# Query weights split one tile earlier, down scales folded into a weight copy, and gate blocks in banks of their own

## The chip, the cores and the metric

The kernel runs on one core of a Trainium2 chip. A core has five engines that work at the same time and meet only at semaphores: TensorE (PE, matrix products into PSUM), VectorE (DVE), ScalarE (ACT), GpSimd (POOL), and SyncE (SP), which here issues every load and store. PSUM has eight banks of 128x512 float32. The metric is the device time of one execution in microseconds, lower is better. Before the change the median of three runs is 315.86 us (315.81 to 316.04).

## The reference

A gated cross attention layer and a gated feed forward layer, over 16 batches of 64 tokens with 256 features:

```
h   = layernorm(x);  q = h@wq;  k, v = h@wk, h@wv;  kc, vc = ctx@wk_ctx, ctx@wv_ctx
q, k = rope(rms_norm(q)*q_w), rope(rms_norm(k)*k_w);  kc = rms_norm(kc)*k_w
p   = softmax(q@[kc,k].T/sqrt(128) + causal mask)       # 16 query heads, 4 key heads
x1  = x + tanh(g_xattn) * (p@[vc,v]).reshape(...)@wo
h2  = layernorm(x1)
a   = silu((h2@fp8(gate_w))*gate_scale) * ((h2@fp8(up_w))*up_scale)     # 768 wide
out = x1 + tanh(g_ffn) * (a@fp8(down_w))*down_scale
```

fp8() rounds a weight to e4m3 and back to float32. The float32 accuracy has to be kept.

## The kernel before

**Tiles and steps.** The tokens are eight tiles of 128 rows (two batches each), and each tile has four head groups. One pair (tile, group) is a step, so there are 32 steps, 0 to 31, and seven more (32 to 38) in which the pipeline drains. Step k is tile k // 4, group j = k % 4. Each engine has its own function `one_step`, and the order of the work is the order in which these functions are written. In step k PE turns the rotated queries of step k (L609), projects the queries of step k + 1 (L625 or L628), applies the output weights to the attention of step k - 2 (`output_projection`), multiplies queries and keys of step k (L664), turns the probabilities of step k - 1 (L676), projects one kind of key or value of the next tile (`keys_values`), does one piece of a feed forward (`FF_LATE`: pieces 0, 1, 2 and the down product of tile t in steps 4t+6 to 4t+9) and ends with the attention product of step k - 1 (L708).

**The softmax loop.** Beside PE there is a loop through the other engines: ACT copies the turned queries (`qt`, L817), squares the projected ones (L739), DVE rotates them (L1035, L1039), takes the row maximum of the scores (L1168) and makes `exp_bias` (L1171), ACT does the exponentials (L897), then the copy of the attention output (`ot_raw` or `ot_hi`, L806 and L810), and again `qt`.

**Native and split weights.** A float32 product by PE is either native (operands as they are, `one_pass`, L411) or split: weight and token matrix are each cut into a high part that is exact in fp32r and a low remainder, and three products (hi x hi, hi x lo, lo x hi; `high_passes` and `low_passes`, L400 and L405) are added up. `NATIVE_TILES` says how many of the first tiles use native products for each kind of weight; later tiles use the split ones. `SPLIT_AT` says in which step a weight chunk is split: ACT copies the high part (`split_weights`, L727, between `pt` and the exponentials of that step), DVE subtracts it from the raw chunk (L957, between `ssq_eps` and `row_inv`). PE waits at the first use for `w_lo_ready`.

**Rounding.** The six feed forward chunks are rounded to e4m3 by DVE (`rounding_constant`, `round_weights`, `out_of_range`), one in each step of `ROUND_AT`. For the two chunks of the down weights POOL writes the result to `w_down` one step later (`quantize_store`, L1315). The first down product, in step 9, waits for both (L532).

**The last tile.** Its feed forward runs in steps 34 to 37. Gate and up blocks of a piece share a bank, its three pieces have the banks ps_f, ps_k, ps_s. ACT makes tanh of the gate block (L793), DVE multiplies it by the gate block (L1051) and by the up block and `fuse_scale` (L1061, two instructions of 128x128), PE does the down product native (L540), DVE multiplies by the row `down_rows` (L1070) and adds x (L1074), and SP stores the tile.

Of the kernel before, what the change touches and what calls it, by code (L numbers as in the profile page):

```python
# [45 lines left out]

NATIVE_TILES = {"kv": (3, 3, 3, 3), "q": (3, 3, 3, 3), "o": (3, 3, 3, 3)}
SPLIT_AT = {5: [("kv", 0)], 6: [("kv", 1)], 7: [("kv", 2)], 9: [("kv", 3)], 10: [("q", 0)], 11: [("q", 1)],
            12: [("q", 2), ("o", 0)], 13: [("q", 3)], 14: [("o", 1)], 15: [("o", 2)], 16: [("o", 3)]}
SPLIT_ORDER = [c for at in sorted(SPLIT_AT) for c in SPLIT_AT[at]]  # L50
ROUND_AT = {0: 0, 1: 1, 2: 2, 3: 3, 4: 4, 8: 5}
NAN_AT = 4
# [8 lines left out]

SHORT_OF_VECTOR = (3,)

# [26 lines left out]
def build(nc, x, ctx_in, wq, wk, wv, wo, wk_ctx, wv_ctx,  # L90
# [5 lines left out]
    with ExitStack() as stack:  # L96
# [6 lines left out]
        def sem(name):  # L103
            return stack.enter_context(nc.semaphore(name))
# [22 lines left out]
        with nc.sbuf_tensor("kv_raw", [P, 4, KC, GW], f32) as kv_raw, \  # L127
# [10 lines left out]
        w_ff = sb("w_ff", [P, 2, KC, FF], f16)  # L138
        w_down = sb("w_down", [P, FC, HID], f32r)
        quant_m = sb("quant_m", [P, FF])  # L140
        ff_peak = sb("ff_peak", [P, WIDE])
# [53 lines left out]


        ident_in, const_in, rows_in, small_in, down_rows_in, x0_in, x1_in, x_in = (
            sem(n) for n in ("ident_in", "const_in", "rows_in", "small_in", "down_rows_in", "x0_in", "x1_in", "x_in"))
# [30 lines left out]
        ff_made, tanh_ready, gated_ready, fuse_ready, fuse_hi_ready, fuse_lo_ready = (  # L229
            sem(n) for n in ("ff_made", "tanh_ready", "gated_ready", "fuse_ready", "fuse_hi_ready", "fuse_lo_ready"))  # L230
        down_made, down_scaled, result_ready = sem("down_made"), sem("down_scaled"), sem("result_ready")

# [162 lines left out]
        def _(pe):  # L395
# [97 lines left out]
            def spread_nan(u, k):  # L493

                if at_step(u, k) == NAN_AT:
# [5 lines left out]
                    last.then_inc(nan_spread, 1)  # L501

            def feed_forward(u, slot):

# [3 lines left out]
                if piece is not None:  # L508
# [7 lines left out]
                    elif piece > 0 and ff_bank(u, ff_m, piece) is ps_f:  # L516
                        pe.wait_ge(fuse_ready, tile(u, ff_m) * 3 + piece)
                    bank_f = ff_bank(u, ff_m, piece)
                    blocks = ((0, 2 * piece), (0, 2 * piece + 1), (1, 2 * piece), (1, 2 * piece + 1))
                    for a in range(2):  # L520
# [202 lines left out]
        def _(act):  # L723
# [60 lines left out]
            def tanh_gate(u, slot):  # L784

                ff_m, piece = slot or (None, None)
                if piece is not None:
                    act.wait_ge(ff_made, tile(u, ff_m) * 3 + piece + 1)
                    if isinstance(u, int) and tile(u, ff_m) == 0 and piece == 0:
# [151 lines left out]
        def _(dve):  # L941
# [77 lines left out]
            def down_row_scale():  # L1019
# [4 lines left out]
                                        ALU.mult, ALU.add).then_inc(scales_ready, 1)  # L1024

            def rotate_queries(u, k):

# [14 lines left out]
            def gate_and_fuse(u, slot):  # L1042
# [4 lines left out]
                if piece is not None:  # L1047
# [9 lines left out]
                    elif piece == 0 and is_tile(u, ff_m - 1):  # L1057
                        dve.wait_ge(result_ready, tile(u, ff_m))
                    for i in range(2):
                        c = 2 * piece + i  # L1060
# [5 lines left out]
                if piece is None:  # L1066
                    dve.wait_ge(down_made, tile(u, ff_m) + 1)
                    if not last_tile(u, ff_m):
                        dve.wait_ge(fuse_lo_ready, tile(u, ff_m) * 3 + 3)
                    nc.vector.tensor_tensor(down_y, ff_bank(u, ff_m, piece)[:, 0:HID], down_rows[:, :], ALU.mult)\  # L1070
                        .then_inc(down_scaled, 1)
                    if last_tile(u, ff_m):
                        dve.wait_ge(down_scaled, tile(u, ff_m) + 1)
                        nc.vector.tensor_tensor(x_tile(u, ff_m), down_y, x_tile(u, ff_m), ALU.add)\  # L1074
                            .then_inc(result_ready, 1)

# [11 lines left out]
            def one_step(u, k):  # L1088
# [122 lines left out]

                split_weights(u, k)

                if at_step(u, k) in ROUND_AT:
# [265 lines left out]
```

## Time and profile before

| | |
|---|---|
| median of three runs | 315.86 us |
| profiled execution, its own time | 316.00 us |
| its span, first to last instruction | 314.0 us |
| PE busy (weight loads) | 296.9 us, 95% (233.1 us) |
| DVE, ACT, POOL busy | 229.0, 232.0, 182.3 us |
| granted clock of PE | full in all 40 slices |

Busy shares of all 314 us say little here, since PE, and the loop through ACT and DVE, take turns at setting the pace. The chain of waits, in order of time, tells which does so in which step. DMA is done with its large loads after the first four of 40 slices (some 31 us) and moves little afterwards. Records of PE overlap a little, since ends of matmuls are modelled, so in the chain a piece is counted from the end of the piece before it.

### The profile page before, as it was taken

What the parts mean: (1) busy time and instruction counts of PE and PEld (TensorE: products, weight loads), DVE (VectorE), ACT (ScalarE), POOL (GpSimd) and SP (SyncE); (2) the same over time, 40 slices, a digit from 0 to 9 for tenths busy, and PEclk for the clock granted to TensorE, in tenths of its full rate; (3) what the DMA queues carried; (4) which work ended last, traced back from release to release, by engine and by line L of the source; (5) the groups of instructions that cost most, each with busy time, mean ns of one, the idle gap of its engine ahead of it and who ended that gap; (6) DMA issues with size and microseconds to landing.
All of it is one profiled execution on the core that took longest, in us unless ns stands there. A gap on an engine that the chain in (4) does not pass through costs nothing.

```text
span 314.0 us, 6534 instructions
## 1 busy us (share of the span) xinstructions
PE 296.9 (95%) x2223; PEld 233.1 (74%) x2223; DVE 229.0 (73%) x478; ACT 232.0 (74%) x892; POOL 182.3 (58%) x177
## 2 busy tenths in 40 slices
PE   7897989998999899999999999999999999987976
PEld 3344656666767678878888888888888888786864
DVE  1668998889759976769887787758765865576554
ACT  2468688777878678897999768896888678776622
POOL 1235685577646877346975586457755684456230
PEclk9999999999999999999999999999999999999999
DMA  6999000000000010000100010000000000000001
GB/s 197 395 390 380 8 17 2 0 1 11 8 2 2 0 35 2 0 0 3 34 2 0 2 37 0 2 1 20 0 3 0 2 18 3 0 2 17 2 0 35
DMA packets 6721, 12.84 MB, mean 41 GB/s; under 512 B 801, under 2 KB 4257, under 8 KB 6689
## 3 DMA queue, kind: packets, MB, share of 16 engines
q1 hardware_dynamic: 6688, 12.43, 11.1%
q8 instruction: 18, 0.29, 0.4%
q14 instruction: 15, 0.11, 0.1%
HBM read 11.38 MB, written 1.05 MB: 40 GB/s over the span
## 4 chain that ended last, share of the span: by engine, by line
PE 35%; ACT 25%; DVE 22%; issue 8%; POOL 6%; DMA 2%; SPq 1%; DVEq 0%; POOLq 0%
ACT probs L897 9%; ACT squares L739 6%; PE ps_y L437 5%; DVE row_max L1168 4%; PE ps_attn L708 3%; DVE exp_bias L1171 3%; PE ps_scores L664 3%; PE ps_transposed L423 3%; DVE q_sin L1039 3%; PE ps_q L411 3%; ACT qt L817 3%; PE ps_ff L525 3%; PE ps_probs L423 2%; DVE q_rot L1035 2%; PE ps_kv L411 2%
## 5 line engine op out<-in xcount | busy, mean ns | idle before, releaser
L897 ACT ACTIVATE probs<-ps_scores,exp_bias,q_scale 128x128 f32<-128x128 f32 x128 | 56.9, 455 | 24.1 <-DVE exp_bias L1171 24.1
L1343 POOL TENSOR_TENSOR q_rot<-q_rot,q_sin 128x512 f32<-128x512 f32 x31 | 39.7, 1279 | 19.1 <-DVE q_sin L1039 18.9
L1387 POOL TENSOR_TENSOR probs<-probs,row_inv 128x512 f32<-128x512 f32 x32 | 36.7, 1146 | 17.9 <-DVE row_inv L1221 17.7
L1294 POOL TENSOR_TENSOR q_scale<-ssq_eps,minus_half 128x4 f32<-128x4 f32 x32 | 40.2, 1255 | 9.7 <-DVE ssq_eps L1194 8.9
L1305 POOL TENSOR_TENSOR fuse_lo<-fuse,fuse_hi 128x256 fp32r<-128x256 f32 x21 | 15.4, 732 | 44.1 <-ACT fuse_hi L748 44.1
L739 ACT ACTIVATE squares<-ps_q 128x128 bf16<-128x128 f32 x128 | 34.0, 292 | 6.7 <-PE ps_q L405 3.9
L708 PE MATMUL ps_attn<-pt,values 128*128 128x256 f32 x128 | 33.4, 383 | 0.0
L664 PE MATMUL ps_scores<-kt,qt 128*64 128x128 f32 x512 | 33.3, 273 | 0.0
L1035 DVE TENSOR_TENSOR q_rot<-ps_q,rope 128x512 f32<-128x512 f32 x31 | 21.2, 685 | 14.0 <-ACT squares L739 14.0
L873 ACT ACTIVATE pt<-ps_probs 128x512 f32<-128x512 f32 x32 | 19.2, 600 | 14.5 <-PE ps_probs L423 14.4
L664 PEld LDWEIGHTS ps_scores<-kt,qt 128*64 128x64 f32 x512 | 28.9, 137 | 0.0
L739 ACT ACTIVATION_READ_ACCUMULATOR squares<-ps_q 128x1 f32 x128 | 27.9, 223 | 0.0
L708 PEld LDWEIGHTS ps_attn<-pt,values 128*128 128x128 f32 x128 | 23.1, 190 | 5.4 <-issue 2.9
L897 ACT ACTIVATION_READ_ACCUMULATOR probs<-ps_scores,exp_bias,q_scale 128x1 f32 x128 | 25.8, 201 | 0.0
L1294 POOL TENSOR_TENSOR k_inv<-k_var,minus_half 128x4 f32<-128x4 f32 x16 | 16.6, 1036 | 13.7 <-DVE k_var L1257 6.4
L411 PE MATMUL ps_q<-q_raw,xt_raw 128*128 128x512 f32 x48 | 22.8, 596 | 1.0 <-DMA q_raw<-in_wq_dram 1.0
L1221 DVE RECIPROCAL row_inv<-row_sum 128x4 f32<-128x4 f32 x32 | 5.6, 175 | 24.4 <-ACT probs L897 24.4
L437 PE MATMUL ps_y<-o_raw,ot_raw 128*128 128x256 f32 x96 | 22.7, 380 | 0.0
L423 PE MATMUL ps_probs<-const,probs 128*128 128x128 f32 x128 | 21.0, 287 | 1.6 <-POOL probs L1387 1.6
L1168 DVE TENSOR_REDUCE row_max<-ps_scores 128x4 f32<-128x512 f32 x32 | 21.8, 680 | 0.2 <-PE ps_scores L664 0.2
L1039 DVE TENSOR_TENSOR q_sin<-ps_q,rope 128x512 f32<-128x512 f32 x31 | 21.1, 679 | 0.0
L739 ACT ACTIVATE squares<-ps_kv 128x128 bf16<-128x128 f32 x60 | 15.9, 291 | 6.3 <-DVE k_sin L1130 3.9
(173 smaller groups left out, 824.0 us busy)
## 6 DMA issues: line engine op xcount, KB each, us to landing
q_raw<-in_wq_dram SPq DMA_DIRECT2D x4, 512.0 KB, 8.7
o_raw<-in_wo_dram SPq DMA_DIRECT2D x4, 512.0 KB, 11.5
ctx_t<-in_ctx_dram SPq DMA_DIRECT2D x8, 128.0 KB, 2.9
out_dram<-x_sb SPq DMA_DIRECT2D x8, 128.0 KB, 2.1
stage<-in_gate_w_dram SPq DMA_DIRECT2D x2, 384.0 KB, 10.5
stage<-in_up_w_dram SPq DMA_DIRECT2D x2, 384.0 KB, 11.4
x_sb<-in_x_dram SPq DMA_DIRECT2D x1, 768.0 KB, 13.4
stage<-in_down_w_dram SPq DMA_DIRECT2D x2, 384.0 KB, 13.0
```

The lines of the kernel that those rows point to most:

```text
L411: last = nc.tensor.matmul(dst, lhs(i), weights[:, i, :], start=(i == 0), stop=(i == KC - 1))
L423: last = nc.tensor.matmul(dst[:, i * P:(i + 1) * P], src, ident, start=True, stop=True, is_transpose=True)
L437: last = nc.tensor.matmul(ps_y[:, 0:HID], ot_raw[:, h, :], o_raw[:, g0, h, :], start=(g0 == 0 and h == 0), stop=(g0 == GROUPS - 1 and h == ...
L664: last = nc.tensor.matmul(scores[r * LEN:(r + 1) * LEN, h, :], qt[:, r, h, :], kt[:, par, j, 2 * r:2 * r + 2, :], start=False, stop=(h == ...
L708: last = nc.tensor.matmul(ps_o[:, r * 256:(r + 1) * 256], values[:, p0, r, g0 * DIM:(g0 + 1) * DIM], pt[:, :].rearrange("p (h r l) -> p r ...
L739: last = nc.scalar.activation(squares[:, h, :], src[:, h * DIM:(h + 1) * DIM], ACT.Square, accum_out=dst[:, h:h + 1])
L897: last = nc.scalar.activation(probs[:, i, :], ps_s[:, i * P:(i + 1) * P], ACT.Exp, bias=exp_bias[:, i:i + 1], scale=q_scale[:, k % 2, i:i ...
L1039: nc.vector.tensor_tensor(halves(q_sin[:, :, :]), rotated(four(ps_q)), halves(over_heads(rope[:, 1, :])), ALU.mult).then_inc(q_sin_ready, 1)
L1168: nc.vector.tensor_reduce(row_max[:, :], four(ps_s), AX.X, ALU.max).then_inc(max_ready, 1)
L1294: return nc.gpsimd.tensor_tensor(dst, src, minus_half[:, 0:src.shape[1]], ALU.pow)
L1343: nc.gpsimd.tensor_tensor(q_rot[:, :, :], q_rot[:, :, :], q_sin[:, :, :], ALU.add)\
L1387: nc.gpsimd.tensor_tensor(probs[:, :, :], probs[:, :, :], row_inv[:, :].unsqueeze(2).broadcast_to([P, 4, P]), ALU.mult).then_inc(probs_rea ...
```

## The change

Four things are changed.

1. Query weights are native for two tiles and no longer for three. So tile 2 (queries projected in steps 7 to 10) uses the split products. Its tokens have to be there in raw form (for the keys and values of that tile, which stay native) and split: one ACT copy and one DVE subtraction of 128x256 are added in step 4. All splits get new steps. Step 6 has two copies, step 8 has three, steps 9 to 14 have one, steps 7, 15 and 16 have none.
2. The last down chunk is rounded in step 7, no longer in step 8, so that POOL writes it in step 8.
3. Last tile: DVE writes `w_last` = down weights x `fuse_scale` (by partition) x `down_rows` (by column), six instructions of 128x256, one in each of steps 24 to 29, into the staging buffer of the gate weights. The scales at L1061 and L1070 go, so that each piece has one product of 128x256, and the end has one addition. Gate and up blocks have banks of their own, the matmuls are ordered gate hi, up hi, gate lo, up lo, and ACT waits for the gate block alone.
4. Step 33: ACT does the tanh of tile 6, piece 2, ahead of the copy `ot_hi`, and DVE does gate and fuse of it ahead of `ot_lo`.

```
-NATIVE_TILES = {"kv": (3, 3, 3, 3), "q": (3, 3, 3, 3), "o": (3, 3, 3, 3)}
-SPLIT_AT = {5: [("kv", 0)], 6: [("kv", 1)], 7: [("kv", 2)], 9: [("kv", 3)], 10: [("q", 0)], 11: [("q", 1)],
-            12: [("q", 2), ("o", 0)], 13: [("q", 3)], 14: [("o", 1)], 15: [("o", 2)], 16: [("o", 3)]}
+NATIVE_TILES = {"kv": (3, 3, 3, 3), "q": (2, 2, 2, 2), "o": (3, 3, 3, 3)}
+SPLIT_AT = {5: [("q", 0)], 6: [("q", 1), ("kv", 0)], 8: [("q", 2), ("q", 3), ("kv", 1)], 9: [("kv", 2)], 10: [("kv", 3)],
+            11: [("o", 0)], 12: [("o", 1)], 13: [("o", 2)], 14: [("o", 3)]}
-ROUND_AT = {0: 0, 1: 1, 2: 2, 3: 3, 4: 4, 8: 5}
+ROUND_AT = {0: 0, 1: 1, 2: 2, 3: 3, 4: 4, 7: 5}
-SHORT_OF_VECTOR = (3,)
+SHORT_OF_VECTOR = (3, STEPS + 1)
+SCALE_DOWN_AT = {STEPS - 2 - FC + c: c for c in range(FC)}
...
+            def feed_last(piece, bank_f):
...
+                pass_of(0, bank_f, 0)
+                pass_of(1, UP_BANK[piece], 0)
+                pe.wait_ge(x2_lo_ready, TILES)
+                pass_of(0, bank_f, 1).then_inc(gate_made, 1)
+                pass_of(1, UP_BANK[piece], 1).then_inc(ff_made, 1)
...
+                    else:
+                        pe.wait_ge(down_weighted, FC)
...
-                                                    w_down[:, c, :].bitcast(f32), start=(c == 0), stop=(c == FC - 1))
+                                                    w_last[:, c, :], start=(c == 0), stop=(c == FC - 1))
...
+                if at_step(u, k) == STEPS + 1:
+                    tanh_gate(u, FF_LATE[k - 1])
...
-                if slot and not last_tile(u, slot[0]):
+                if slot and not last_tile(u, slot[0]) and at_step(u, k) != STEPS + 1:
...
+            def scale_down_weights(c):
...
+                nc.vector.scalar_tensor_tensor(w_last[:, c, :], w_down[:, c, :].bitcast(f32), fuse_scale[:, c:c + 1],
+                                               down_rows[:, :], ALU.mult, ALU.mult).then_inc(down_weighted, 1)
...
+                    if last_tile(u, ff_m):
+                        dve.wait_ge(ff_made, count)
+                        nc.vector.tensor_tensor(fuse_part(u, ff_m, piece).rearrange("p a n -> p (a n)"),
+                                                gated.rearrange("p a n -> p (a n)"), UP_BANK[piece][:, 0:2 * P], ALU.mult)\
+                            .then_inc(fuse_ready, 1)
+                        return
...
+                    if last_tile(u, ff_m):
+                        nc.vector.tensor_tensor(x_tile(u, ff_m), ff_bank(u, ff_m, piece)[:, 0:HID], x_tile(u, ff_m), ALU.add)\
+                            .then_inc(result_ready, 1)
+                        return
...
+                if at_step(u, k) in SCALE_DOWN_AT:
+                    scale_down_weights(SCALE_DOWN_AT[step(u, k)])
```

ACT, step 8 up to the `qt` of step 9, before (the line numbers of the changed kernel differ: L897 is its L932, L727 its L756):

```order
L873 ACTIVATE pt<-ps_probs 128x512
L897 ACTIVATE probs,row_sum<-ps_scores,exp_bias,q_scale 128x128 x4
L806 ACTIVATE ot_raw<-ps_attn 128x2x4x64
L817 ACTIVATE qt<-ps_transposed 128x512
L739 ACTIVATE squares,k_ssq<-ps_kv 128x128 x4
```

and in the changed kernel:

```order
L908 ACTIVATE pt<-ps_probs 128x512
L756 ACTIVATE q_hi<-q_raw 128x1024 x2
L756 ACTIVATE kv_hi<-kv_raw 128x1024
L932 ACTIVATE probs,row_sum<-ps_scores,exp_bias,q_scale 128x128 x4
L841 ACTIVATE ot_raw<-ps_attn 128x2x4x64
L852 ACTIVATE qt<-ps_transposed 128x512
```

Three copies of 128x1024 now stand between `pt` and the exponentials. Before there was none in this step.

POOL, from step 8 into step 9, before (`w_down` is the rounded down weights, `q_scale` the scale of the next step's queries):

```order
L1343 TENSOR_TENSOR q_rot<-q_rot,q_sin 128x512
L1294 TENSOR_TENSOR q_scale<-ssq_eps,minus_half 128x4
L1387 TENSOR_TENSOR probs<-probs,row_inv 128x512
L1294 TENSOR_TENSOR k_inv<-k_var,minus_half 128x4
L1305 TENSOR_TENSOR fuse_lo<-fuse,fuse_hi 128x256
L1343 TENSOR_TENSOR q_rot<-q_rot,q_sin 128x512
L1315 TENSOR_TENSOR w_down<-stage,quant_m 128x768
```

and in the changed kernel (L1367 is the write of `w_down`, L1395 the sum of `q_rot`):

```order
L1395 TENSOR_TENSOR q_rot<-q_rot,q_sin 128x512
L1367 TENSOR_TENSOR w_down<-stage,quant_m 128x768
L1346 TENSOR_TENSOR q_scale<-ssq_eps,minus_half 128x4
L1439 TENSOR_TENSOR probs<-probs,row_inv 128x512
L1346 TENSOR_TENSOR k_inv<-k_var,minus_half 128x4
L1357 TENSOR_TENSOR fuse_lo<-fuse,fuse_hi 128x256
L1395 TENSOR_TENSOR q_rot<-q_rot,q_sin 128x512
```

The write of the second half of `w_down` moved up by five instructions, a whole step, and stands now ahead of `q_scale` and `probs` of step 8.

DVE, the last tile from its first gate product to the end, before:

```order
L1051 SCALAR_TENSOR_TENSOR const<-const,ps_ff 128x256
L1061 SCALAR_TENSOR_TENSOR fuse<-const,fuse_scale,ps_ff 128x128 x2
L1051 SCALAR_TENSOR_TENSOR probs<-probs,ps_kv 128x256
L1061 SCALAR_TENSOR_TENSOR k_cos<-probs,fuse_scale,ps_kv 128x128 x2
L1051 SCALAR_TENSOR_TENSOR probs<-probs,ps_scores 128x256
L1061 SCALAR_TENSOR_TENSOR k_cos<-probs,fuse_scale,ps_scores 128x128 x2
L1070 TENSOR_TENSOR fuse<-ps_q,down_rows 128x256
L1074 TENSOR_TENSOR x_sb<-fuse,x_sb 128x256
```

and in the changed kernel (ps_attn, ps_probs and ps_y hold the up blocks):

```order
L1094 SCALAR_TENSOR_TENSOR const<-const,ps_ff 128x256
L1104 TENSOR_TENSOR fuse<-const,ps_attn 128x256
L1094 SCALAR_TENSOR_TENSOR probs<-probs,ps_kv 128x256
L1104 TENSOR_TENSOR k_cos<-probs,ps_probs 128x256
L1094 SCALAR_TENSOR_TENSOR probs<-probs,ps_scores 128x256
L1104 TENSOR_TENSOR k_cos<-probs,ps_y 128x256
L1120 TENSOR_TENSOR x_sb<-ps_q,x_sb 128x256
```

Eleven instructions have become seven: three pairs became one instruction each, and the product by `down_rows` is gone.

## Rows read from the trace of the kernel before

**Rows 1.** Chain of waits, steps 7 to 14: start us, us, engine and work.

```profile
79.34 1.72 PE ps_q L411 x4
...
106.19 1.69 PE ps_ff L545 x12
...
118.25 1.17 PE ps_q L400 x4
...
127.39 0.93 PE ps_q L400 x4
128.32 0.47 PE ps_q L405 x2
...
143.03 1.42 PE ps_ff L545 x12
...
145.76 0.33 issue
```

**Rows 2.** Timeline of PE, step 9: start us, us, engine, line, work, [idle before <-releaser].

```profile
104.22 0.63 PE L405 MATMUL ps_kv<-kv_hi,xt_lo 128*128 128x512 f32 x2
106.19 0.39 PE L545 MATMUL ps_ff<-w_down,fuse_hi 128*128 128x256 f32 x1 [1.34 <-POOL w_down L1315]
```

**Rows 3.** Timeline of ACT, step 12, the one step with two weight copies.

```profile
132.46 0.60 ACT L873 ACTIVATE pt<-ps_probs 128x512 f32<-128x512 f32 x1 [0.79 <-PE ps_probs L423]
132.96 1.05 ACT L727 ACTIVATE q_hi<-q_raw 128x1024 fp32r<-128x1024 f32 x1
133.90 1.05 ACT L727 ACTIVATE o_hi<-o_raw 128x1024 fp32r<-128x1024 f32 x1
...
136.59 0.61 ACT L806 ACTIVATE ot_raw<-ps_attn 128x512 f32<-128x512 f32 x1
```

**Rows 4.** Timeline of PE, start of step 13.

```profile
137.31 1.94 PE L437 MATMUL ps_y<-o_raw,ot_raw 128*128 128x256 f32 x8
```

**Rows 5.** Timeline of ACT, `qt` of steps 16 and 17.

```profile
163.72 0.61 ACT L817 ACTIVATE qt<-ps_transposed 128x512 f32<-128x512 f32 x1
172.06 0.61 ACT L817 ACTIVATE qt<-ps_transposed 128x512 f32<-128x512 f32 x1
```

**Rows 6.** Timeline of DVE: step 5, then `row_inv` of step 25.

```profile
62.10 0.17 DVE L1118 TENSOR_SCALAR k_var<-k_ssq 128x4 f32<-128x4 f32 x1 [0.26 <-ACT squares L739]
...
249.30 0.18 DVE L1221 RECIPROCAL row_inv<-row_sum 128x4 f32<-128x4 f32 x1 [0.60 <-ACT probs L897]
```

**Rows 7.** Line L1171, all its instructions: ns min/median/max, first and last start.

```profile
L1171 DVE SCALAR_TENSOR_TENSOR exp_bias<-row_max,q_scale x32: 161/727/755, 23.1 to 292.5; 128x4 f32<-128x4 f32 x32
```

**Rows 8.** Timeline of ACT, step 33.

```profile
298.98 0.60 ACT L810 ACTIVATE ot_hi<-ps_attn 128x512 fp32r<-128x512 f32 x1 [0.89 <-PE ps_attn L708]
299.48 0.62 ACT L793 ACTIVATE const<-ps_q,tanh_scale 128x128 f32<-128x128 f32 x2
```

**Rows 9.** Timeline of DVE, steps 34 to 38.

```profile
303.37 0.42 DVE L1098 TENSOR_SCALAR xn<-x_sb,x_mean,x_inv 128x256 f32<-128x256 f32 x1 [0.67 <-POOL x_inv L1294]
...
307.26 0.61 DVE L1061 SCALAR_TENSOR_TENSOR fuse<-const,fuse_scale,ps_ff 128x128 f32<-128x128 f32 x2
...
311.03 0.42 DVE L1070 TENSOR_TENSOR fuse<-ps_q,down_rows 128x256 f32<-128x256 f32 x1 [1.22 <-PE ps_q L540]
311.49 0.42 DVE L1074 TENSOR_TENSOR x_sb<-fuse,x_sb 128x256 f32<-128x256 f32 x1
```

**Rows 10.** Timeline of PE, steps 33 to 37.

```profile
302.67 0.36 PE L545 MATMUL ps_ff<-w_down,fuse_hi 128*128 128x256 f32 x1 [1.36 <-POOL fuse_lo L1305]
...
304.17 0.38 PE L423 MATMUL ps_transposed<-const,xn 128*128 128x128 f32 x2
...
307.28 0.61 PE L525 MATMUL ps_scores<-x2t_lo,w_ff 128*128 128x128 f16 x8
307.92 1.13 PE L540 MATMUL ps_q<-w_down,fuse 128*128 128x256 f32 x4
308.89 2.11 PE L540 MATMUL ps_q<-w_down,k_cos 128*128 128x256 f32 x8
```

More of the change, by code:

```diff
@@ L139, in build @@
         w_down = sb("w_down", [P, FC, HID], f32r)
+        w_last = stage[:, 0:2, :].rearrange("p a n -> p (a n)").rearrange("p (c n) -> p c n", c=FC)
         quant_m = sb("quant_m", [P, FF])
@@ L194, in build @@
             bank(n) for n in ("ps_transposed", "ps_q", "ps_scores", "ps_attn", "ps_ff", "ps_kv", "ps_y", "ps_probs"))
+        UP_BANK = (ps_o, ps_p, ps_y)
         ident_in, const_in, rows_in, small_in, down_rows_in, x0_in, x1_in, x_in = (
@@ L230, in build @@
             sem(n) for n in ("ff_made", "tanh_ready", "gated_ready", "fuse_ready", "fuse_hi_ready", "fuse_lo_ready"))
+        down_weighted, gate_made = sem("down_weighted"), sem("gate_made")
         down_made, down_scaled, result_ready = sem("down_made"), sem("down_scaled"), sem("result_ready")
@@ L501, in spread_nan, with pass_of @@
                     last.then_inc(nan_spread, 1)
+            def feed_last(piece, bank_f):
+                def pass_of(w, bank, a):
+                    for i in range(2):
+                        for kc in range(KC):
+                            c = 2 * piece + i
+                            last = nc.tensor.matmul(bank[:, i * P:(i + 1) * P], w_ff[:, w, kc, c * P:(c + 1) * P],
+                                                    x2t[a][:, (TILES - 1) % 2, kc, :], start=(a == 0 and i == 0 and kc == 0),
+                                                    stop=(a == 1 and kc == KC - 1), skip_group_check=True)
+                    return last
+                pass_of(0, bank_f, 0)
[3 more added lines that the diff above has]
+                pass_of(1, UP_BANK[piece], 1).then_inc(ff_made, 1)
             def feed_forward(u, slot):
@@ L518, in feed_forward @@
                     bank_f = ff_bank(u, ff_m, piece)
+                    if last_tile(u, ff_m):
+                        feed_last(piece, bank_f)
+                        return
                     blocks = ((0, 2 * piece), (0, 2 * piece + 1), (1, 2 * piece), (1, 2 * piece + 1))
@@ L787, in tanh_gate @@
                 if piece is not None:
-                    act.wait_ge(ff_made, tile(u, ff_m) * 3 + piece + 1)
+                    if last_tile(u, ff_m):
+                        act.wait_ge(gate_made, piece + 1)
+                    else:
+                        act.wait_ge(ff_made, tile(u, ff_m) * 3 + piece + 1)
                     if isinstance(u, int) and tile(u, ff_m) == 0 and piece == 0:
@@ L1024, in down_row_scale @@
                                         ALU.mult, ALU.add).then_inc(scales_ready, 1)
+            def scale_down_weights(c):
+                if c == 0:
+                    dve.wait_ge(quant_done, WIDE + 2)
+                    dve.wait_ge(scales_ready, 3)
+                nc.vector.scalar_tensor_tensor(w_last[:, c, :], w_down[:, c, :].bitcast(f32), fuse_scale[:, c:c + 1],
+                                               down_rows[:, :], ALU.mult, ALU.mult).then_inc(down_weighted, 1)
             def rotate_queries(u, k):
@@ L1058, in gate_and_fuse @@
                         dve.wait_ge(result_ready, tile(u, ff_m))
+                    if last_tile(u, ff_m):
+                        dve.wait_ge(ff_made, count)
[3 more added lines that the diff above has]
+                        return
                     for i in range(2):
@@ L1069, in gate_and_fuse @@
                         dve.wait_ge(fuse_lo_ready, tile(u, ff_m) * 3 + 3)
+                    if last_tile(u, ff_m):
+                        nc.vector.tensor_tensor(x_tile(u, ff_m), ff_bank(u, ff_m, piece)[:, 0:HID], x_tile(u, ff_m), ALU.add)\
+                            .then_inc(result_ready, 1)
+                        return
                     nc.vector.tensor_tensor(down_y, ff_bank(u, ff_m, piece)[:, 0:HID], down_rows[:, :], ALU.mult)\
                         .then_inc(down_scaled, 1)
[L1072 to L1075, printed above, removed]
             def attention_low(u, k):
```

## The prediction, made before the changed kernel had run

> **What bounds the kernel now.** I read the chain of waits first, in order of time. From step 6 to step 15 it runs almost only over PE, piece after piece, so there a microsecond less on PE, or a stall less, is a microsecond less of time. Two things break it. In step 9 it leaves PE for POOL: PE sits idle for 1.34 us in front of the first down product, released by POOL's write of `w_down` [rows 2]. At the end of step 13 it idles 0.33 us before a split query projection [rows 1]. Then I read the distance from one `qt` to the next. From step 16 on the loop through ACT and DVE sets the pace: step 16 takes 172.06 - 163.72 = 8.34 us [rows 5], and PE is nearly full beside it. That part is not touched and should keep its length. Last come the timelines of steps 33 to 37, where everything is serial and each piece that goes is time. PE's granted clock is full throughout, with idle stretches of over a microsecond in it, so I leave the clock out.
>
> **The sum's frame.** Durations are from the profiled execution, 316.00 us by its own time (span 314.0 and 2.0 around it). The median of the runs, 315.86, lies 0.14 lower.
>
> **Query products of tile 2.** A native projection (two float32 matmuls of 512 columns, each two passes in the records) takes 1.72 us. A split one takes 0.93 for the high passes and 0.47 for the low, 1.40 [rows 1]. Four projections, in steps 7 to 10, all in the PE-bound stretch: 4 x 0.32 = 1.28 us gained.
>
> The Trainium skill says (FP8 and Floating Point Precision, section TensorE Precision Notes) that a true float32 product needs four passes through the array. Three fp32r products against four would be a saving of a quarter, 0.43 of 1.72 instead of 0.32, and a gain of 1.72. The row differs from that, and the sum goes by the row.
>
> **The down chunk one step earlier.** In step 9 the chain goes from the end of the low passes of the value projection, 104.22 + 0.63 = 104.85 [rows 2], to the end of the down product, 106.19 + 1.69 = 107.88 [rows 1], which is 3.03 us. The same product without a wait takes 1.42 [rows 1]. So 1.61 us go. What is late next there is the low part of `fuse`, some microseconds earlier. POOL's write (1.8 us by the chain) now delays `q_scale` and `probs` of step 8, which PE needs only after the scores of step 9. DVE does the rounding (five instructions) in step 7, where it loses one subtraction and had idle time; it ends about when the queries of step 8 are squared. I cost that at nothing. Without cover it would be 0.3 to 0.6.
>
> **Splits ahead of their use.** Before, two query chunks were split one step before PE needed them, and their low parts came late. At 145.76 PE idles 0.33 us; and the high passes that follow a late weight take 1.17 instead of 0.93, as at 118.25 [rows 1]. Together 0.24 + 0.33 + 0.24 = 0.81 us. In the new table those chunks are ready steps ahead. Gained: 0.81.
>
> **Three copies in step 8.** This is the cost. In step 12 ACT had two copies. From the start of `pt` at 132.46 to the end of `ot_raw` at 136.59 + 0.61 = 137.20 it took 4.74 us, and PE started on `ps_y` at 137.31, just in time [rows 3, 4]. Steps 8 and 12 are the same kind of step (j = 0), with the same PE work between those points in the new kernel. A third copy adds 133.90 - 132.96 = 0.94 us [rows 3], so `ot_raw` ends at 138.14 in step 12's times, and PE starts 0.87 later than 137.31 (with 0.04 for the semaphore). Bounds: 0 if PE had unseen slack, 1.9 if both copies beyond the first came on the path, as they do on the loop of ACT. I take 0.87, the row it is nearest to. The single copies of steps 9 to 14 fit into the gap in which ACT waits for `exp_bias`, as before. Step 6 has two, with PE about 1 us behind them: nothing.
>
> **Two small pushes.** The low part of the tokens in step 4 is one more DVE instruction (about 0.35 us on its queue), ahead of a `k_var` that has 0.26 of idle time before it [rows 6]: 0.1. In step 9 ACT is late by the three copies, so the key scaling on DVE comes some 0.2 after PE could turn the keys. I subtract 0.3 for both (from 0 to 0.8). The copy on ACT in step 4 fits in a gap.
>
> Middle of the kernel: 1.28 + 1.61 + 0.81 - 0.87 - 0.3 = 2.53 us. Checked against the loop: PE's own work of steps 10 to 13 is then longer than the loop, and from step 14 on the loop's paces (8.3 to 8.8) take over. I find no place where it takes more than about 0.1 of this away.
>
> **The six products of the weight copy.** SCALAR_TENSOR_TENSOR, 128x256, some 0.42 us each by its neighbours of that size (L1074 has 0.42 too) [rows 9]. They stand before `row_inv`, where DVE idles for the exponentials. The tightest of the six places are steps 25 and 29, with 0.60 us idle [rows 6]. So nothing, and 6 x 0.42 = 2.5 us if nothing covered them.
>
> Here a row warns. `exp_bias`, a SCALAR_TENSOR_TENSOR on 128x4 numbers, takes 161 ns at best and 727 in the median [rows 7]; the long ones lie beside a large sum on POOL. A product held up like that would take 0.42 + 0.57, about 1.0, and not fit in 0.60. But at its place in steps 25 and 29 POOL does only small powers. The Trainium skill has the rule (SBUF — State Buffer, section Who interferes with whom): a DVE instruction with two SBUF inputs contends with a GpSimd one that reads SBUF, and the second to issue blocks until the first ends. By that rule, the trace agrees, both operands of the new products count; the rival that follows is priced below.
>
> **Step 33.** ACT idles 0.89 us before `ot_hi` and the tanh takes 0.62 [rows 8], so it fits ahead. Gate and fuse of DVE then come 1.5 us earlier, `ot_lo` at most 0.1 later, which PE does not need yet. The down product of tile 6, which started at 302.67 after 1.36 us of idling, can follow `ps_y` at once, and ends (1.7 us of work) by 303.0. The turn of the last tile's tokens was queued behind it and started at 304.17, though `xn` was ready at 303.37 + 0.42 = 303.79 [rows 9, 10]. With 0.15 for the handover it starts at 303.95: gained 0.22, no more, since `xn` is what is late next.
>
> **Steps 34 to 38.** Gate blocks ready 0.23 us earlier, since four of sixteen matmuls come after them; two products of 0.61 become one of 0.42 [rows 9]. DVE's last `fuse` then comes 0.57 earlier. But PE has six float32 matmuls to do, in three pairs. They start at 307.92 and 308.89 [rows 10], 0.97 apart and each cold, since it waited for its `fuse`. If they follow one another from the end of the blocks (307.89, [rows 10]) and stay 0.97 apart, the gain is 0.2; if they run on without the cold start, 0.5. I take 0.5, since the first `fuse` will be there before PE is free. The removal of L1070 saves 311.49 - 311.03 = 0.46 [rows 9]. Together 0.22 + 0.5 + 0.46 = 1.18 us.
>
> **Sum.** 316.00 - 2.53 - 1.18 = 312.29 in terms of the profiled execution; by the median, 312.15. I predict 312.2 us.
>
> **Rivals.**
>
> A. The forecast, 312.2, own range 311.6 to 312.8: chance 0.60.
>
> B. The three copies cost the loop of ACT and DVE all of their two extra lengths, 1.9 and 0.16 for the cold start, and not 0.87, because the loop and PE are nearly equal and nothing is recovered afterwards. 1.2 us less gain: 313.4. For it: `ot_raw`, `qt` and two sets of squares stand behind the copies. Against it: steps 9 to 13 have native output products and PE was behind the loop there. Chance 0.16.
>
> C. DVE and POOL collide. In step 8 the write of `w_down` (1.8) runs as DVE starts the first of three subtractions, and in step 6 a second subtraction can keep `ln_inv` waiting. That is 0.3 to 0.4 us each beyond what I covered: 312.9. Chance 0.11. For it: the spread of L1171 [rows 7].
>
> D. The end does not get shorter than 0.2, because PE's float32 products bound it and something replaces L1070's time, so that this part doesn't do what it says: 313.2. Chance 0.05.
>
> E. Slower. The six products on DVE are not covered: each is held by a POOL instruction, 1.0 us, and then holds up `row_inv`, `ot_lo` and the loop. It decides against the change from 3.7 / 6 = 0.62 us on the path for each. In full: 312.2 + 6.0 = 318.2. Against it: 1.0 us would have to find no idle time at six places, and the tightest has 0.60. Chance 0.03.
>
> F. More gain: the copies cost nothing and the tail gives 0.1 more: 311.3. Chance 0.05.
>
> **How the numbers follow.** A, C and the nearer parts of B, D and F lie between 311.2 and 313.8, which leaves out under 2 in 10. What a measurement of this kernel can tell from no change is 0.2%, 0.6 us. A, B, C, D and F are all faster by more (B by 2.5 us). Faster 0.94, same 0.03 (E partly covered, or B with C and D together), slower 0.03.
>
> **What the profile afterwards would show.** PE's idle before L545 of step 9 (its L574) is gone. Four more query projections read 1.40. In step 9 PE idles 0.7 to 0.9 us before `ps_y`, released by ACT's `ot_raw`. There is no late `w_lo` in steps 10 and 13. `qt` of step 16 starts some 2.5 us earlier than at 163.72, and the pace afterwards is 8.34 again. DVE's idle before `row_inv` in steps 24 to 29 is shorter by 0.4, and `row_inv` is no later against the exponentials. From `qt` of step 31 to the end it is 1.2 us less. I am wrong if the stall in step 9 is over 1.5 us or comes again in steps 10 to 12, or if the pace after step 16 changes.

## The result, and the profile after

| | before | after |
|---|---|---|
| median (range), 4 runs each on the same chip | 315.84 us (315.77 to 316.04) | 312.27 us (312.23 to 312.65) |
| ratio, 95% interval | | 0.9887 (0.9875 to 0.9898) |
| profiled execution, its own time | 316.00 us | 312.29 us |
| its span | 314.0 us | 310.2 us |

The prediction was 312.2 us, and the kernel is 1.1% faster. Single runs of one kernel on one chip lie up to 1.8 us apart, most of the long ones at a granted clock of 0.993 to 0.995, so differences below 1 us are read from the traces. The page of the changed kernel, part 1 and the row of the granted clock of part 2:

```profile
PE 294.8 (95%) x2231; PEld 234.8 (76%) x2231; DVE 229.4 (74%) x481; ACT 232.2 (75%) x893; POOL 180.8 (58%) x177
...
PEclk9999999999999999999999999999999999999999
```

Shares of busy time have hardly moved, and the clock is full as before. What moved is read from the starts of `qt`. Here is the first one of step 7, then those of steps 16 and 31. First the kernel before (its step 16 is in [rows 5]), timeline of ACT:

```profile
79.43 0.59 ACT L817 ACTIVATE qt<-ps_transposed 128x512 f32<-128x512 f32 x1
...
289.70 0.59 ACT L817 ACTIVATE qt<-ps_transposed 128x512 f32<-128x512 f32 x1
```

and the changed kernel:

```profile
79.38 0.59 ACT L852 ACTIVATE qt<-ps_transposed 128x512 f32<-128x512 f32 x1
...
160.94 0.61 ACT L852 ACTIVATE qt<-ps_transposed 128x512 f32<-128x512 f32 x1
...
169.27 0.61 ACT L852 ACTIVATE qt<-ps_transposed 128x512 f32<-128x512 f32 x1
...
287.05 0.59 ACT L852 ACTIVATE qt<-ps_transposed 128x512 f32<-128x512 f32 x1
```

| stretch, us | before | after | difference |
|---|---|---|---|
| `qt` of step 7 to `qt` of step 16 ("middle") | 84.29 | 81.56 | -2.73 |
| step 16 to step 31 | 125.98 | 126.11 | +0.13 |
| step 31 to the end of the span ("end") | 24.33 | 23.12 | -1.21 |

The pace of the loop is the same, 169.27 - 160.94 = 8.33 against 8.34 [rows 5]. The 0.13 is no effect of the change: a second profile of the same changed kernel has 125.93.

Now to the place where the idle time was [rows 2]. The chain of waits of the changed kernel, from step 8 into step 9 (start us, us, what):

```profile
92.96 0.60 PE ps_probs L430 x4
93.58 0.60 ACT pt L908
94.18 1.89 ACT q_hi L756 x2
96.08 0.95 ACT kv_hi L756
97.02 1.76 ACT probs L932 x8
98.78 0.49 ACT ot_raw L841
99.28 0.48 ACT qt L852
...
103.72 0.94 PE ps_kv L407 x4
104.65 0.46 PE ps_kv L412 x2
105.12 1.42 PE ps_ff L574 x12
```

The down product (now L574) follows at once and takes 1.42; the 1.34 us in front of it are gone. The chain now leaves PE earlier, for ACT: the three copies stand on it. How much PE loses there is in its timeline, from the turn of the queries to the output product of step 9:

```profile
96.60 0.60 PE L430 MATMUL ps_transposed<-const,q_rot 128*128 128x128 f32 x4
97.61 0.47 PE L407 MATMUL ps_q<-q_hi,xt_hi 128*128 128x512 f32 x1 [0.41 <-issue]
...
98.61 0.63 PE L412 MATMUL ps_q<-q_hi,xt_lo 128*128 128x512 f32 x2
99.33 1.99 PE L444 MATMUL ps_y<-o_raw,ot_raw 128*128 128x256 f32 x8
```

Where nothing is late, as in step 10, the high passes start 0.36 us after the turn and `ps_y` 1.84 us after it (107.24, 107.60 and 109.08). Here that would be 96.96 and 98.44, so `ps_y` is 0.9 late. But 0.65 of it lies before the query projection, and that does not wait for ACT's `ot_raw`. The timelines of DVE and POOL show for what, the first `q_lo` and the write of `w_down`:

```profile
95.16 2.34 DVE L992 TENSOR_TENSOR q_lo<-q_raw,q_hi 128x1024 fp32r<-128x1024 f32 x1 [0.44 <-ACT q_hi L756]
```

```profile
94.58 1.84 POOL L1367 TENSOR_TENSOR w_down<-stage,quant_m 128x768 fp32r<-128x768 f32 x1
96.38 2.01 POOL L1346 TENSOR_TENSOR q_scale<-ssq_eps,minus_half 128x4 f32<-128x4 f32 x1
```

`q_lo` ends at 97.50, 1.08 after POOL's write ends, and PE starts 0.11 later. Two things stand in step 9, then: `q_lo`, which makes the projection 0.65 late, and the copies of ACT, behind which `ot_raw` ends at 99.28, 0.05 before `ps_y` starts. I call such a limit a wall. The experiments take the two apart.

The end, timeline of PE and then of DVE, for [rows 8 to 10]:

```profile
298.48 0.34 PE L574 MATMUL ps_ff<-w_down,fuse_hi 128*128 128x256 f32 x1
...
301.17 0.44 PE L430 MATMUL ps_transposed<-const,xn 128*128 128x128 f32 x2 [1.02 <-DVE xn L1147]
...
304.78 1.08 PE L569 MATMUL ps_q<-stage,fuse 128*128 128x256 f32 x4
305.70 1.89 PE L569 MATMUL ps_q<-stage,k_cos 128*128 128x256 f32 x8
```

```profile
300.70 0.41 DVE L1147 TENSOR_SCALAR xn<-x_sb,x_mean,x_inv 128x256 f32<-128x256 f32 x1 [0.67 <-POOL x_inv L1346]
...
305.87 0.42 DVE L1104 TENSOR_TENSOR k_cos<-probs,ps_y 128x256 f32<-128x256 f32 x1
307.63 0.42 DVE L1120 TENSOR_TENSOR x_sb<-ps_q,x_sb 128x256 f32<-128x256 f32 x1 [1.34 <-PE ps_q L569]
```

The down product of tile 6 has no idle time ahead of it, the turn follows `xn` (301.11) after 0.06, the fp32 products (L569) run from 304.78 to 307.59 without a break, and one addition ends it.

### The profile page after: what moved, and what is told of

Same layout as the page of the kernel before. It is cut to its first block, busy times and chain, and to the rows that moved or that the text cites. A ratio compares the mean times of both kernels' runs of the same rounds, so it can differ in the third digit from the quotient of the medians.

```text
span 310.2 us, 6558 instructions
## 1 busy us (share of the span) xinstructions
PE 294.8 (95%) x2231; PEld 234.8 (76%) x2231; DVE 229.4 (74%) x481; ACT 232.2 (75%) x893; POOL 180.8 (58%) x177
## 4 chain that ended last, share of the span: by engine, by line
PE 31%; ACT 27%; DVE 25%; issue 8%; POOL 6%; DMA 2%; SPq 1%; DVEq 0%; POOLq 0%
ACT probs L932 10%; ACT squares L768 6%; PE ps_y L444 5%; DVE row_max L1217 4%; DVE exp_bias L1220 3%; DVE q_sin L1082 3%; PE ps_attn L737 3%; PE ps_transposed L430 3%; ACT qt L852 3%; PE ps_scores L693 3%; DVE q_rot L1078 2%; PE ps_kv L418 2%; ACT const L825 2%; PE ps_probs L430 2%; DMA const<-in_constants_dram 2%
## 5 line engine op out<-in xcount | busy, mean ns | idle before, releaser
L932 ACT ACTIVATE probs<-ps_scores,exp_bias,q_scale 128x128 f32<-128x128 f32 x128 | 57.0, 456 | 26.5 <-DVE exp_bias L1220 26.4
L1395 POOL TENSOR_TENSOR q_rot<-q_rot,q_sin 128x512 f32<-128x512 f32 x31 | 39.7, 1281 | 17.6 <-DVE q_sin L1082 17.5
L1346 POOL TENSOR_TENSOR q_scale<-ssq_eps,minus_half 128x4 f32<-128x4 f32 x32 | 38.8, 1213 | 10.5 <-DVE ssq_eps L1243 9.8
L932 ACT ACTIVATION_READ_ACCUMULATOR probs<-ps_scores,exp_bias,q_scale 128x1 f32 x128 | 25.8, 202 | 0.0
L407 PE MATMUL ps_q<-q_hi,xt_hi 128*128 128x512 f32 x48 | 20.9, 436 | 0.4 <-issue 0.4
```

What stands on the lines that cost most here:

```text
L932: last = nc.scalar.activation(probs[:, i, :], ps_s[:, i * P:(i + 1) * P], ACT.Exp, bias=exp_bias[:, i:i + 1], scale=q_scale[:, k % 2, i:i ...
L1346: return nc.gpsimd.tensor_tensor(dst, src, minus_half[:, 0:src.shape[1]], ALU.pow)
L1395: nc.gpsimd.tensor_tensor(q_rot[:, :, :], q_rot[:, :, :], q_sin[:, :, :], ALU.add)\
```

## Experiments

Each kernel was timed beside the kernel before on its chip, and the ratio is to that. The medians of the kernel before went from 315.84 to 316.66 us over the chips, so the medians of two rows aren't to be subtracted. Differences below 1 us are taken from the traces, by the stretches of the table above. They begin at `qt` of step 7, which lies anywhere from 79.26 to 80.75 us in these traces, so what happens earlier stays out.

| kernel | median us | ratio to before (95%) | middle | end |
|---|---|---|---|---|
| before | 315.84 | 1 | 84.29 | 24.33 |
| rounding in step 7 alone | 314.73 | 0.9944 (0.9922 to 0.9965) | 82.67 | 24.33 |
| the three tables alone | 313.34 | 0.9894 (0.9874 to 0.9915) | 81.54 | 24.34 |
| changed | 312.27 | 0.9887 (0.9875 to 0.9898) | 81.56 | 23.12 |
| changed, queries native again | 313.27 | 0.9911 (0.9887 to 0.9935) | 82.72 | 23.12 |
| changed, rounding in step 8 | 317.41 | 1.0029 (1.0012 to 1.0046) | 85.98 | 23.13 |
| changed, four copies in step 8 | 313.32 | 0.9896 (0.9874 to 0.9918) | 82.48 | 23.16 |
| changed, key chunk 1 in step 7 | 312.22 | 0.9866 (0.9841 to 0.9891) | 81.20 | 23.16 |
| changed, query chunk 2 in step 7 | 311.22 | 0.9845 (0.9827 to 0.9863) | 80.60 | 23.15 |
| changed, products twice | 312.70 | 0.9884 (0.9862 to 0.9906) | 81.55 | 23.12 |
| changed, order of step 33 back | 312.65 | 0.9878 (0.9859 to 0.9897) | 81.55 | 23.43 |
| changed, tanh waits for both blocks | 312.17 | 0.9872 (0.9854 to 0.9889) | 81.54 | 23.27 |
| changed, once more | 312.51 | 0.9888 (0.9867 to 0.9910) | 81.53 | 23.15 |

**The rounding alone.**

```
-ROUND_AT = {0: 0, 1: 1, 2: 2, 3: 3, 4: 4, 8: 5}
+ROUND_AT = {0: 0, 1: 1, 2: 2, 3: 3, 4: 4, 7: 5}
```

> The kernel before with the last down chunk rounded in step 7, nothing else. My theory: the idle time of PE before the first down product of step 9 (1.34 us) goes, 1.61 us of chain with the rest that it cost, and there are no three copies beside it: 314.2 us, and qt of step 10 about 1.6 earlier. Rival: without the copies PE reaches step 9 earlier, and something else is then late there (the write of w_down delays q_scale and with it the rotated queries, as in the changed kernel, where q_lo took 2.34 us beside POOL's write): a gain of 0.8 to 1.2 only, 314.6 to 315.0.

The middle is 84.29 - 82.67 = 1.62 us shorter. My theory held: without copies nothing else is late in step 9. The interval of the times (1.1 to 2.5 us) leaves the rival's 1.2 open; the trace does not.

**The three tables alone** (the first three edits of the diff, on the kernel before).

> The kernel before with the three tables of the change alone (queries native for two tiles, the new places of the splits, the last down chunk rounded in step 7); the end of the kernel is the old one. My theory (middle and end add up, 2.7 and about 1.1 us by the places of qt in the two traces): 315.8 - 2.65 = 313.2 us, qt of step 16 some 2.8 us earlier than before, and from qt of step 31 to the end the same time as before, within 0.1. Rival: the two parts are not independent, and a part of the gain seen behind step 31 was carried there from the middle: then it is below 312.9.

81.54 and 24.34: the middle is that of the full change and the end that of the kernel before. So the gain splits into 2.75 and 1.21 with nothing carried from one to the other. Against the rounding alone, the split products and new places bring 82.67 - 81.54 = 1.13.

**Queries native again, old places of the splits, in the changed kernel.**

```
-NATIVE_TILES = {"kv": (3, 3, 3, 3), "q": (2, 2, 2, 2), "o": (3, 3, 3, 3)}
+NATIVE_TILES = {"kv": (3, 3, 3, 3), "q": (3, 3, 3, 3), "o": (3, 3, 3, 3)}
```

(and `SPLIT_AT` as before)

> The changed kernel with queries native for three tiles again and the old places of the splits; the rounding in step 7 and the new end stay. My theory: the products' 1.28 and the late weights' 0.81 go, the stall of the three copies (0.9) and the small pushes go as well: 312.3 + 1.1 = 313.4 us. Rival (the split products and early splits brought much more, since the middle gained 2.7 with the stall in it): 314.0 or more. Rival (nearly all the gain of the middle is the rounding): 312.5 or less.

+1.16 in the middle. The same 1.1 from both sides, as the theory had it.

**Key chunk 1 in step 7: one copy fewer in step 8.**

```
-            ... 8: [("q", 2), ("q", 3), ("kv", 1)], 9: [("kv", 2)], ...
+            ... 7: [("kv", 1)], 8: [("q", 2), ("q", 3)], 9: [("kv", 2)], ...
```

> The changed kernel with the copy and subtraction of key chunk 1 in step 7 in place of step 8, so that ACT has one copy in step 7 and two in step 8. My theory: the stall of PE in step 9 is the third copy's 0.94 us and goes: 312.3 - 0.85 = 311.4 us, no new idle time in step 8. Rival 1 (the stall in step 9 is the subtraction q_lo held by POOL's write of w_down, which stands before the turned queries, and not the copies): 312.1 to 312.3. Rival 2 (DVE in step 7 has rounding and subtraction, and row_inv or q_scale of the next step is late): no gain or a loss, 312.2 to 312.8.

The middle is only 0.36 shorter. My theory, that the stall is the third copy, fell as far as it says that taking the copy away takes the stall away. The timelines of PE and of DVE:

```profile
97.30 0.60 PE L430 MATMUL ps_transposed<-const,q_rot 128*128 128x128 f32 x4
98.58 0.47 PE L407 MATMUL ps_q<-q_hi,xt_hi 128*128 128x512 f32 x1 [0.68 <-issue]
```

```profile
95.86 2.61 DVE L992 TENSOR_TENSOR q_lo<-q_raw,q_hi 128x1024 fp32r<-128x1024 f32 x1 [0.16 <-ACT q_hi L756]
```

`ot_raw` was there in time, but `q_lo` took 2.61 us and ended at 98.47, and `ps_y` is as late as in the changed kernel. What was gained is behind it: ACT is no longer late, and the turn of the keys in step 9 starts 0.50 us after that of `probs`, without a wait (0.70 in the changed kernel). Rival 1 was right on the place, and its gain (0 to 0.2) too small.

But the edit made a part of this wall itself. From `qt` of step 7 to POOL's write of `w_down` it is 15.20 us in the changed kernel and 15.48 here (80.08 to 95.56): DVE has rounding and a subtraction in step 7, and POOL comes later. So `q_lo` ends that much later, and the projection is 0.92 late and no longer 0.65. With the write in its old place, removing one copy would have brought about 0.25 more (an estimate from these numbers).

**Rounding in step 8, in the changed kernel.** The edit of the first experiment, the other way round.

> The changed kernel with the last down chunk rounded in step 8 as before, where DVE now has three subtractions of 128x1024 as well. My theory: the wait for w_down in step 9 comes back (1.6 us of chain, less the 0.9 by which PE is late there anyway), and the rounding behind or ahead of three subtractions (1.1 to 2.3 us each) makes it or q_scale of step 9 later still: 313.5 to 315.5 us, middle 314.5. Rival (PE's lateness through the copies hides the wait for w_down fully): 312.3 to 312.7.

Neither theory: 4.42 us more in the middle than in the changed kernel, where I had 1.2 to 3.2, and slower than before (1.0012 to 1.0046). The timelines of DVE and of PE, steps 8 and 9:

```profile
95.18 2.36 DVE L992 TENSOR_TENSOR q_lo<-q_raw,q_hi 128x1024 fp32r<-128x1024 f32 x2 [0.44 <-ACT q_hi L756]
97.45 1.22 DVE L992 TENSOR_TENSOR kv_lo<-kv_raw,kv_hi 128x1024 fp32r<-128x1024 f32 x1
...
99.77 0.96 DVE L1010 TENSOR_TENSOR stage<-stage,quant_m 128x768 f32<-128x768 f32 x1
100.65 0.17 DVE L1273 RECIPROCAL row_inv<-row_sum 128x4 f32<-128x4 f32 x1
```

```profile
97.98 0.63 PE L412 MATMUL ps_q<-q_hi,xt_lo 128*128 128x512 f32 x2
99.34 1.99 PE L444 MATMUL ps_y<-o_raw,ot_raw 128*128 128x256 f32 x8 [0.73 <-ACT ot_raw L841]
...
102.68 0.66 PE L430 MATMUL ps_probs<-const,probs 128*128 128x128 f32 x4 [0.24 <-POOL probs L1439]
104.98 0.66 PE L430 MATMUL ps_transposed<-const,k_sin 128*128 128x128 f32 x4 [1.65 <-DVE k_sin L1187]
...
109.29 0.39 PE L574 MATMUL ps_ff<-w_down,fuse_hi 128*128 128x256 f32 x1 [2.25 <-POOL w_down L1367]
```

The rounding stands behind three subtractions, and `row_inv` and `k_var` behind parts of the rounding. So the turn of `probs`, the turn of the keys and the down product are late one after the other: 0.24 + 1.65 + 2.25 us. This run also isolates ACT's wall. Without `w_down` beside it the two `q_lo` take 2.36 together and PE starts its projection without a wait; yet `ps_y` starts at 99.34, as in the changed kernel (99.33, and `qt` of step 7 at 79.40 and 79.38). So the hold on `q_lo` costs the changed kernel nothing, and the copies alone make the 0.9. The hold is the lower wall, 0.65; with one copy less and the write pushed back, it alone makes 0.9.

**Four copies in step 8.**

```
-            ... 8: [("q", 2), ("q", 3), ("kv", 1)], 9: [("kv", 2)], ...
+            ... 8: [("q", 2), ("q", 3), ("kv", 1), ("kv", 2)], ...
```

> The changed kernel with the copy and subtraction of key chunk 2 moved from step 9 to step 8, so that ACT has four copies of 128x1024 between pt and the exponentials there, and none in step 9. My theory: each further copy is on the path with its 0.94 us: 313.2 us, PE's ps_y of step 9 0.9 later. Rival (the copies cost the loop twice, as my case B had it): 314.1. Rival (they are hidden, the stall is from the DVE side): 312.3 to 312.5.

The middle is 0.92 longer: one copy is one copy's 0.94 us. Not hidden and not twice, so case B's mechanism isn't there.

**Query chunk 2 in step 7: both walls gone.**

```
-            ... 8: [("q", 2), ("q", 3), ("kv", 1)], 9: [("kv", 2)], ...
+            ... 7: [("q", 2)], 8: [("q", 3), ("kv", 1)], 9: [("kv", 2)], ...
```

> The changed kernel with the copy and subtraction of query chunk 2 in step 7 (in place of step 8), so that step 8 splits only query chunk 3 and key chunk 1. Behind it stand two readings of what is late in step 9. Reading 1, my theory now: two walls of the same height stand there, ACT's third copy ahead of ot_raw and DVE's subtraction q_lo of chunk 2, which POOL's write of w_down holds (2.34 us in place of 1.23); moving the key chunk took away only the first, moving query chunk 2 takes away both, and ps_y of step 9 starts 0.9 us earlier: from qt of step 7 to qt of step 16 the time is 81.56 - 0.9 = 80.6 to 80.8 us (81.20 with the key chunk moved), the whole 0.9 below the changed kernel. Reading 2: a further split in step 7 delays DVE's q_rot there, and POOL's write with it, and that alone is what PE meets in step 9: as with the key chunk moved, 81.2, 0.4 below the changed kernel.

Reading 1: the middle is 80.60, 0.96 shorter. The timelines of PE and of DVE:

```profile
96.83 0.48 PE L407 MATMUL ps_q<-q_hi,xt_hi 128*128 128x512 f32 x1
...
98.31 1.94 PE L444 MATMUL ps_y<-o_raw,ot_raw 128*128 128x256 f32 x8
```

```profile
95.04 2.62 DVE L992 TENSOR_TENSOR q_lo<-q_raw,q_hi 128x1024 fp32r<-128x1024 f32 x1 [0.16 <-ACT q_hi L756]
```

A `q_lo` held for 2.62 us is still there, but it is now that of chunk 3, which PE wants a step later. What reading 2 named happens too, POOL's write comes 15.48 us after `qt` of step 7, but PE doesn't meet it. Not all is gone: the turn of the keys still starts 0.70 us after that of `probs` (101.28 and 101.98). This version is the fastest: 311.22 against 312.51 us of the changed kernel on the same chip (fastest runs 311.13 and 312.07).

**The products of the weight copy twice.** Each instruction of `scale_down_weights` is issued a second time behind the first, writing the same numbers again.

> The changed kernel with each of the six products that write w_last done twice on DVE, one after the other (0.42 us more in each of steps 24 to 29). My theory: DVE idles before row_inv in these steps, and what stood there is not used up: 0 to 0.2 in the tight steps 25 and 29, none in the others, 312.3 to 312.7 us. Rival (DVE is on the loop there, the first product was only just covered): 6 x 0.42 = 2.5 more, 314.8 us.

No cost: step 16 to 31 takes 126.07 (126.11 and 125.93 in the two profiles of the changed kernel). DVE's timeline in the tight step 25, the changed kernel and then this one:

```profile
245.88 0.47 DVE L1066 SCALAR_TENSOR_TENSOR stage<-w_down,fuse_scale,down_rows 128x256 f32<-128x256 f32 x1
246.58 0.18 DVE L1273 RECIPROCAL row_inv<-row_sum 128x4 f32<-128x4 f32 x1 [0.22 <-ACT probs L932]
```

```profile
247.10 0.48 DVE L1070 SCALAR_TENSOR_TENSOR stage<-w_down,fuse_scale,down_rows 128x256 f32<-128x256 f32 x1
247.50 0.17 DVE L1277 RECIPROCAL row_inv<-row_sum 128x4 f32<-128x4 f32 x1
...
254.63 1.27 DVE L1070 SCALAR_TENSOR_TENSOR stage<-w_down,fuse_scale,down_rows 128x256 f32<-128x256 f32 x1
```

The idle time is used up in step 25, and still nothing is lost. In step 26 one product was held beside a POOL product of 128x512 (`k_sin`, from 254.57) and took 1.27; what case E named does happen, and the idle time there (1.48 us before `row_inv` in the changed kernel, 0.17 left here) takes it.

**Order of step 33 back.**

```
-SHORT_OF_VECTOR = (3, STEPS + 1)
+SHORT_OF_VECTOR = (3,)
```

(and ACT's tanh behind `ot_hi` again)

> The changed kernel with the order of step 33 as before: ACT copies ot_hi ahead of the tanh of tile 6, DVE does ot_lo ahead of gate and fuse. My theory: the turn of the last tile's tokens waits again behind the down product of tile 6, 0.22 to 0.27 us: 312.5 us. Rival (xn is what everything waits for, and the order is worth nothing): 312.3 us, the same to 0.05.

The end is 0.28 to 0.31 longer (23.43 against 23.12 and 23.15). The wait is back, in PE's timeline:

```profile
300.01 0.36 PE L574 MATMUL ps_ff<-w_down,fuse_hi 128*128 128x256 f32 x1 [1.39 <-POOL fuse_lo L1355]
...
301.51 0.38 PE L430 MATMUL ps_transposed<-const,xn 128*128 128x128 f32 x2
```

**The tanh waits for both blocks.** ACT waits for `ff_made` in place of `gate_made`.

> The changed kernel in which ACT waits for both blocks of a piece (gate and up) of the last tile before its tanh, and not for the gate block alone; banks and order of the matmuls stay. My theory: every fuse comes 0.23 us later, but PE is still at the up blocks and then at the fp32 products, each pair 0.92 us, and the second and third fuse were there 0.29 and 0.35 us before PE asked for them: at most 0.05 us more, and 0.2 at the first pair if fuse of piece 0 comes after 304.78; 0 to 0.1. Rival: the last tile is a chain through ACT and DVE, and the whole 0.23 to 0.3 comes on top.

The end is 0.12 to 0.15 longer, a little over the bound, and half of what the rival had. In this kernel the first `fuse` ends at 304.56 and the first fp32 product starts 0.15 later:

```profile
304.14 0.42 DVE L1101 TENSOR_TENSOR fuse<-const,ps_attn 128x256 f32<-128x256 f32 x1
```

Only the first pair feels it, as I had it. Of the end's 1.21 us the early tanh is about 0.13, step 33 about 0.3, and what remains, about 0.8, is with the removed L1070 and the shorter `fuse`. Those two were not run apart; by the trace L1070 is 0.46 of it (311.03 to 311.49, [rows 9]).

**The changed kernel once more.**

> The changed kernel as it is, beside the others of this call, so that they can be compared on one chip. Expected: 0.9887 of the kernel before, within 0.1%, and 81.56 us from qt of step 7 to qt of step 16.

0.9888 and 81.53: as expected.

## Why the prediction was right, step by step

| term | predicted | measured | by |
|---|---|---|---|
| down chunk one step earlier | 1.61 | 1.62 | rounding alone against before |
| query products, early splits, the two small pushes | 1.28 + 0.81 - 0.3 = 1.79 | 2.07 | rounding alone (82.67) against query chunk 2 in step 7 (80.60) |
| of these: query products | 1.28 | 1.28 | PE of the same two traces, steps 7 to 10 |
| of these: early splits | 0.81 | 0.87 | the same, steps 11 and 14 |
| of these: key turn of step 9 later | -0.2 | -0.32 | the same, step 9 |
| of these: key turn of step 13 earlier | 0 | 0.32 | the same, step 13 |
| of these: push in step 4 | -0.1 | 0 | starts of `qt` up to step 7 |
| of these: taken back by the loop, steps 15 and 16 | 0 | -0.08 | the rest up to `qt` of step 16 |
| three copies in step 8 | -0.87 | -0.96 | query chunk 2 in step 7 against changed |
| middle | 2.53 | 2.73 | trace before and after |
| six products | 0 | 0 | products twice |
| step 33 | 0.22 | 0.3 | its order back |
| fp32 products and blocks, L1070 | 0.96 | 0.9 | the rest of the end |
| end | 1.18 | 1.21 | trace before and after |

**Right.** The sum and its large terms. The reading that carried most was that in steps 7 to 14 the chain runs over PE, so that durations of PE's pieces [rows 1] add up. The four split projections read 0.93 or 0.94 and 0.46 or 0.47 in the chain, and in steps 10 and 13 none is late. Case A's mechanism is what happened.

**Mis-sized.** The middle is 0.2 us better, and it is in the row of products, splits and pushes, 2.07 for 1.79. The products brought what I had. Of the pushes the one in step 4 cost nothing: up to step 7 the starts of `qt` are earlier by 0.05 in the changed kernel, so the `k_var` with 0.26 of idle time [rows 6] was not on the path. The one in step 9 is there and is larger, since the pieces beside the turn take longer too. What the sum left out is the same push in the kernel before, in step 13. PE there, before:

```profile
140.28 0.66 PE L423 MATMUL ps_probs<-const,probs 128*128 128x128 f32 x4
140.98 0.66 PE L423 MATMUL ps_transposed<-const,k_sin 128*128 128x128 f32 x4
```

and in the changed kernel:

```profile
138.29 0.66 PE L430 MATMUL ps_probs<-const,probs 128*128 128x128 f32 x4
138.78 0.60 PE L430 MATMUL ps_transposed<-const,k_sin 128*128 128x128 f32 x4
```

Before, the two copies of step 12 had ACT just in time for `ps_y` [rows 3, 4], and `k_sin`, which comes behind ACT's squares, late: DVE's record of it ends at 140.92 and the turn starts 0.06 later. The changed kernel has one copy in step 12, and the wait is gone; in the run with the old places of the splits it is back (0.71 between the two starts). From the turn of the queries of step 13 to that of step 14 PE takes 9.37 us, before 9.69. I used these two copies as the model of what step 9 would cost, and didn't see that step 13 already paid and would get it back. A product of the weight copy is 0.47 us and not 0.42. In step 33 I took 0.15 for the handover from `xn` to PE, and it is 0.06.

**Luck.** The sum, 312.29, agrees with the profiled execution to the last digit, and that is chance. The middle gave 0.20 more than I had, the end 0.03 and the start 0.05; against it the loop took 0.13 longer in this profile, and the time outside the span grew from 1.97 to 2.12 us.

**Right in size, incomplete in cause.** I said that PE would idle 0.7 to 0.9 us before `ps_y`, released by `ot_raw`. `ps_y` is 0.9 late, but most of the idle time lies before the query projection, behind `q_lo`. I had `q_lo` held by `w_down` as case C, at 0.3 to 0.4 on top. It is not on top: it lies in the shadow of the copies, as the run with the rounding in step 8 shows (same start of `ps_y`, `q_lo` not held). And its price was too low: it is 0.65 high in the changed kernel, and 0.92 where a split in step 7 pushes POOL's write back.

**What a sum of terms hid.** The rounding is worth 1.62 us alone and 4.42 in the changed kernel, since three subtractions moved into its old step. The edits are only additive in the order in which I took them; without the second edit, the rest would have been slower than before.

**The rule on shared ports.** The Trainium skill (SBUF — State Buffer, section Who interferes with whom) says that a DVE instruction with two SBUF inputs and a GpSimd one that reads SBUF exclude each other for the whole instruction. For the large write the traces agree: `q_lo` takes 1.23 us with POOL idle, and beside `w_down` it ends 1.08, 1.09 and 1.10 us after POOL's write does, whatever its start (95.16, 95.86, 95.04). For POOL's small powers they don't: `q_scale` on 128x4 numbers ran from 245.78 for 1.01 us in the changed kernel, and DVE's product that began beside it at 245.88 took 0.47 us, like its five others (0.47 or 0.48). The rule alone would have had it wait.

## What to carry to other kernels

A stall has the height of its tallest wall: before you remove what the chain names, look in the other engines' timelines for what ends just before it, and move the thing that feeds both (here one chunk, 0.96 us instead of 0.36). Look too at what the moved work delays where it goes. Where the chain runs over one engine alone, its pieces add up, here to 0.1 us. When one step is your model for what another will cost, ask whether the change takes that cost away in the first. Where work is moved into a step, price the edits in the order in which they depend on each other, since the one that makes room can be worth far more than alone. Work put into DVE's idle time was free here even where it filled it (step 25), since DVE was waiting for ACT there.

## What the runs showed of the hardware

- A DVE subtraction of 128x1024 takes 1.22 or 1.23 us alone and 2.34 to 2.62 when POOL's write of 128x768 began before it; it doesn't share the time, it ends 1.1 us after POOL. The other side pays too: POOL's `q_scale` on 128x4 numbers took 2.01 us beside the subtractions and 1.02 with the write of `w_down` elsewhere.
- POOL's small powers (128x4) did not hold DVE: a subtraction of 128x1024 begun at 95.18 us beside `q_scale` (94.81 to 95.83, rounding in step 8) took 1.23 us as alone.
